# A two-layer cross-attention block: its MLP products in float32r halves, with weight blocks streamed through a ring

## What is computed

```
h = ln(x, ln1);  x = x + attn(rope(h@sa_wq), rope(h@sa_wk), h@sa_wv, causal) @ sa_wo
h = ln(x, ln2);  x = x + attn(rope(h@ca_wq), rope(ctx@ca_wk), ctx@ca_wv) @ ca_wo
h = ln(x, ln3);  x = x + gelu_tanh(h @ fc1_w + fc1_b) @ fc2_w + fc2_b        # MLP of layer 0
a = attn(x@Wq.T, ctx@Wk.T, ctx@Wv.T, causal) + x
a = ln(a, ln_g, ln_b);  out = a + gelu(a @ W1.T + b1) @ W2.T + b2            # MLP of layer 1
```

## Time and profile before

| | |
|---|---|
| median of 3 runs | 1115.44 us (1106.16 to 1116.03) |
| the profiled execution | 1116.21 us, of which the span from first to last instruction is 1114.4 us |
| mean granted TensorE clock | 0.917 of full speed |
| PE / DVE / ACT / POOL busy | 83% / 52% / 38% / 7% |
| DMA | 44.05 MB in packets, mean 40 GB/s |

### The profile page before, as it was taken

The page is one execution under the profiler, slowest core; times in us unless marked ns, Lnnn a source line. Parts: engine busy times, 40 slices in busy tenths (PEclk is TensorE's granted clock), DMA queues, the critical chain, the costliest instruction groups (busy, mean ns, idle before and its releaser), DMA issues.

```text
span 1114.4 us, 13662 instructions
## 1 busy us (share of the span) xinstructions
PE 930.4 (83%) x5120; PEld 456.5 (41%) x5120; DVE 582.7 (52%) x1347; ACT 419.9 (38%) x822; POOL 73.2 (7%) x83
## 2 busy tenths in 40 slices
PE   3878774899988898788989867999887898988898
PEld 1533332345443363344445324533233454543365
DVE  5565727774677604488546775666135515325500
ACT  1233321352455616353422422267752333233421
POOL 2101000000000200000000001000000000000210
PEclk9778866799999998988999988999997999996999
DMA  8804463102122200645020401023004004040000
GB/s 285 101 14 61 83 139 43 16 1 29 27 33 30 29 1 20 95 54 62 1 29 9 50 15 15 20 41 38 1 20 57 2 1 57 2 52 8 1 19 19
DMA packets 47012, 44.05 MB, mean 40 GB/s; under 512 B 13510, under 2 KB 44386, under 8 KB 46434
## 3 DMA queue, kind: packets, MB, share of 16 engines
q1 hardware_dynamic: 46948, 43.19, 24.2%
HBM read 13.53 MB, written 2.10 MB: 14 GB/s over the span
## 4 chain that ended last, share of the span: by engine, by line
PE 57%; DVE 17%; DMA 10%; ACT 7%; SPq 5%; issue 4%; ACTq 0%; DVEq 0%
PE ps_o L963 10%; PE ps_exp L851 10%; PE ps_misc L834 9%; PE ps_max L888 8%; DVE mcol L1113 4%; ACT probs L1199 4%; PE ps_exp L921 4%; SPq L695 4%; DMA QA<-part 4%; PE ps_chain L813 3%; PE ps_chain L821 2%; DVE swap L1027 2%; DMA KA<-part 2%; PE ps_exp L926 2%; PE ps_chain L786 2%
## 5 line engine op out<-in xcount | busy, mean ns | idle before, releaser
L1113 DVE TENSOR_REDUCE mcol<-ps_max 128x3 f32<-128x462 f32 (+5 forms) x496 | 292.1, 626 | 176.7 <-PE ps_max L890 101.0
L1199 ACT ACTIVATE probs<-ps_exp 128x512 f32<-128x512 f32 (+3 forms) x544 | 261.1, 523 | 248.2 <-PE ps_exp L924 90.0
L888 PE MATMUL ps_max<-KA,QA 96*128 96x512 bf16 (+3 forms) x384 | 117.3, 357 | 57.7 <-DVE mcol L1113 27.3
L921 PE MATMUL ps_exp<-QA,KA 98*128 98x512 bf16 (+3 forms) x384 | 119.5, 348 | 27.0 <-ACT probs L1199 18.3
L834 PE MATMUL ps_misc<-hT,w_up 128*128 128x512 f32 x256 | 123.5, 605 | 7.2 <-ACT hid L1190 2.2
L851 PE MATMUL ps_exp<-w_down,hid 128*128 128x256 f32 x512 | 127.7, 386 | 0.0
L1190 ACT ACTIVATE hid<-ps_misc,col 128x512 f32<-128x512 f32 x64 | 44.0, 687 | 196.5 <-PE ps_misc L834 196.5
L851 PEld LDWEIGHTS ps_exp<-w_down,hid 128*128 128x128 f32 x512 | 94.1, 190 | 29.7 <-issue 15.3
L1247 POOL TENSOR_TENSOR part<-rot,part 128x512 bf16<-128x512 f32 (+1 forms) x36 | 40.9, 1135 | 916.3 <-DVE part L1037 916.3
L888 PEld LDWEIGHTS ps_max<-KA,QA 96*128 96x128 bf16 x384 | 39.1, 103 | 126.6 <-DVE mcol L1113 68.2
L963 PE MATMUL ps_o<-probs,V 128*17 128x512 f32 (+3 forms) x768 | 84.2, 512 | 2.9 <-ACT probs L1199 2.0
(11 more groups left out here) (109 smaller groups left out, 986.9 us busy)
## 6 DMA issues: line engine op xcount, KB each, us to landing
QA<-part SPq DMA_DIRECT2D x72, 128.0 KB, 5.2
QC<-part SPq DMA_DIRECT2D x72, 128.0 KB, 5.2
KA<-part SPq DMA_DIRECT2D x48, 128.0 KB, 5.1
xb<-in_x SPq DMA_DIRECT2D x8, 512.0 KB, 6.1
out<-xb SPq DMA_DIRECT2D x4, 512.0 KB, 3.0
KC<-part SPq DMA_DIRECT2D x24, 77.0 KB, 3.0
w_up<-in_fc SPq DMA_DIRECT2D x1, 1024.0 KB, 7.9
w_down<-in_fc SPq DMA_DIRECT2D x1, 1024.0 KB, 8.2
```

The lines of the kernel that those rows point to most:

```text
L888: mm = pe.matmul(dst, q, kk, start=True, stop=not causal)
L921: mm = pe.matmul(bank[:, q0:CH], KA[:, g // NT, hh, (g % NT) * P:(g % NT + 1) * P], QA[:, hh, q0:CH], start=True, stop=(r < 0))
L1113: dve.tensor_reduce(dst, src, AX.X, ALU.max).then_inc(s_max_done, 1)
L1199: act.activation(probs[:, n % 2, h, q0:CH], ps_exp[exp_nth[s] % 2][:, q0:CH], ACT.Exp).then_inc(s_exp_done, 1)
```

## The change

The two MLP products are no longer made of float32 matmuls. Each operand is written as a high half in type float32r plus a low half (the difference), and a product becomes three float32r products: high by high, weight low by input high, weight high by input low.

- Weights: a new thread `split_weights()` with priority -3 (ahead of all others) loads the 16 weight blocks two at a time into `stage`, has ACT write the high halves into `ring` and POOL the low halves, and writes both to a DRAM buffer `keep` (8 rounds of one 512 KB load, one ACT and one POOL operation on 128x1024, one 1 MB store). The loads and stores are issued by ACT's queue, which also waits for them. At the end `fetch` brings the first four blocks (512 KB each) into the ring. The loads of all MLP weights at L645, L646, L670 and L671 are gone.
- Every later block is fetched by SP in the place of a `down`, once that down has released the slot: block n+4 after down n.
- `up`: six products of 128x512 into a bank of `ps_chain`. ACT makes the gelu twice, into `hid` (high, float32r) and into the float32 tile `gel`; POOL subtracts to give the low half, then signals `s_low`. There is one `gel`: the next write waits for POOL.
- `down`: eight products with the high half of `hid`, then after `s_low` four with the low half.
- `tr` of ln3 and ln4: ACT makes four activations in place of two (high half into `hup`, full value into `gel`), POOL the low half. Up 0 waits until ACT has done all of it, and its last two products until POOL has.
- The next MLP's `tr` may stand only after the last up of the MLP before it.
- `lnout` moves from POOL (8 operations) to DVE (2 operations on 128x1024), behind up 0.

```diff
+def split_weights():
+    out = [("wload", 0), ("wload", 1), ("wsplit", 0)]
+    for i in range(NSPLIT):
+        out += [("wsplit", i + 1)] * (i + 1 < NSPLIT) + [("wsave", i)] + [("wload", i + 2)] * (i + 2 < NSPLIT)
+    return out + [("fetch",)]
...
         # SP
-            sp.dma_start(w_up[0][:, :, :], fcw[0]).then_inc(s_wrest, 16)
-            sp.dma_start(w_down[0][:, :, :], fcw[1]).then_inc(s_wrest, 16)
...
-                elif k == "late":
-                    after_chain(sp, ("ctxk", 1, KT - 1))
-                    sp.dma_start(w_up[1][:, :, :], fcw[2]).then_inc(s_wlate, 16)
-                    sp.dma_start(w_down[1][:, :, :], fcw[3]).then_inc(s_wlate, 16)
...
+                elif k == "down" and up_nth[("up", *s[1:])] + RING <= len(ups):
+                    n = up_nth[("up", *s[1:])] + RING
+                    block_used(sp, ups[n - RING - 1])
+                    sp.dma_start(ring[:, n % RING, :, :].bitcast(F32), keep[l * NM + m]).then_inc(s_fetched[n % RING], 16)
...
         # PE
+                    pe.wait_ge(s_fetched[n % RING], 16 * ((n - 1) // RING + 1))
+                    bank = chain_bank(s)
+                    for i, j in ((0, 0), (1, 0), (0, 1)):
+                        if m == 0 and j:
+                            pe.wait_ge(s_low, low_nth[("tr", ("ln3", "ln4")[l], c, NT // 2 - 1)])
                     for t in range(KT):
-                        mm = pe.matmul(bank[:, :], w_up[l][:, t, m * P:(m + 1) * P], hT_of("up", c)[:, t, :],
+                            mm = pe.matmul(bank[:, :], ring[:, n % RING, i, t * P:(t + 1) * P], hup[:, j, t, :],
...
+                    pe.wait_ge(s_gelu, n)
                     for t in range(NT):
-                        mm = pe.matmul(dst, hid[:, m % 2, t * P:(t + 1) * P], w_down[l][:, m, :],
+                        for j in range(2):
+                            pe.matmul(dst[t], hid[:, n % 2, 0, t * P:(t + 1) * P], ring[:, n % RING, j, 2 * P:4 * P],
+                    pe.wait_ge(s_low, low_nth[("up", l, c, m)])
+                    for t in range(NT):
+                        mm = pe.matmul(dst[t], hid[:, n % 2, 1, t * P:(t + 1) * P], ring[:, n % RING, 0, 2 * P:4 * P],
...
         # ACT
+                elif k == "wsplit":
+                    act.wait_ge(s_staged[i % 2], 16 * (i // 2 + 1))
+                    if i > 1:
+                        act.wait_ge(s_saved[i % 2], 16 * (i // 2))
+                    act.activation(ring[:, 2 * (i % 2):2 * (i % 2) + 2, 0, :], stage[:, i % 2, :, :], ACT.Copy)
+                elif k == "wsave":
+                    act.wait_ge(s_wlow, i + 1)
+                    act.dma_start(keep[2 * i:2 * i + 2], ring[:, 2 * (i % 2):2 * (i % 2) + 2, :, :])
...
-                    act.activation(hid[:, m % 2, :], ps_misc[:, :], (ACT.Gelu_apprx_tanh, ACT.Gelu)[l],
+                    act.activation(hid[:, n % 2, 0, :], bank[:, :], gelu, bias=bias).then_inc(s_gelu, 1)
+                    act.wait_ge(s_low, low_nth[s] - 1)
+                    act.activation(gel[:, :], bank[:, :], gelu, bias=bias).then_inc(s_chain_free[u % 2], 1)
...
         # POOL
+                elif k == "up":
+                    after_chain(pool, s)
+                    pool.tensor_tensor(hid[:, n % 2, 1, :], gel[:, :], hid[:, n % 2, 0, :],
+                                       ALU.subtract).then_inc(s_low, 1)
```

225 lines of the change are left out of this document (163 added, 62 removed).

## The result

The changed kernel takes 1097.36 us (median of 14 runs, 1091.97 to 1105.48), the kernel before 1115.28 us (14 runs beside it). The ratio is 0.9849, with a 95% interval of 0.9824 to 0.9873: 1.5% faster. The forecast was 1085 with a range from 1056 to 1116, so the range held and the size was off: 18 us came in place of 31. The executions of one kernel differ by 13 to 17 us, the longer ones mostly at a lower granted clock, so a difference of a few us between two single traces is weak evidence by itself. The profiled execution has a span of 1093.3 us against 1114.4, 21.1 less, and all that follows is read against these 21.1.

What follows compares the result with a forecast made beforehand. PE was taken as the bound, with the MLP's matmuls nearly all on the path. Terms -55 + 11 + 4 + 3 + 2 + 2 + 8 - 6 = -31 took 1116.2 us to 1085, range 1056 to 1116.

Steps and rivals of the forecast that it cites:

- passes, 64 pairs: MLP products on PE: up 1.72 to 1.29 us, down 1.73 to 1.30, over 64 pairs: -55 us.
- heads: Start of each MLP: ACT's extra activations delay up 0, +8 us at seven heads and +3 at the last: +11.
- tails, ring, POOL, lnout: MLP tails waiting for low halves +4, POOL behind DVE +3, ring refills +2, `lnout` on DVE +2.
- prologue and reload: Weight split at the start +8 (ACT +5, KA placement +3), x reload without the two 1 MB loads -6.
- rival 4: Products cheaper than a pass, bounded by bf16's 0.23 us per 512 columns; idleness covers heads and tails: 1066 us, chance 0.12.
- One pass, not two: MLP products: a float32r product takes one pass over its columns; two passes would give over 1200 us, chance 0.02.
- The ring's +2: Block refills during MLPs: they fit by 1.7 us, but a `place` between two holds the second: +2 (0 to 22).
- POOL behind VectorE: First MLP: low half of up 2 stands behind the third part of a projection: +3 us (0 to 6).
- The -6 for the reload: x reload at 150 us: the two 1 MB loads ahead go, 12.42 us against a median of 6.1: -6.
- Rival 1: MLPs: waits for ring refills at the 6.1 us end (+20) eat the gain: 1105 us, chance 0.15.
- Rival 2: Prologue: the weight split fills it, +30 rather than +8: 1107 us, chance 0.10.
- Rival 3: Downs: weight loads bind them, above 0.15 us per product; at 0.216 a down takes 2.59 us: 1164 us, chance 0.07.

Runs made afterwards that it cites:

- e6: Changed kernel with the full-precision input of the MLP heads written into the `hT` slot used before the change, not into `gel`: 1085.62 us, 0.9762.
- e12: Edits of e6, e9 and e10 together, with the halves kept as packed bfloat16 tiles in place of float32r: 1071.72 us, 0.9616.
- e4: Changed kernel without the 60 ring refills; all MLPs read the first four blocks, so the output differs: 1093.1 us, 0.9831.
- e9: On top of e6, in POOL's program alone, a projection's last subtraction goes behind an MLP's next subtraction at two places: 1085.48 us, 0.9769.
- e10: On top of e6, VectorE's two `lnout` operations wait for the low half of the input: 1084.52 us, 0.9749.
- e1: Changed kernel with only four of sixteen weight blocks split, after the second row step, and used by all MLPs: 1093.82 us, 0.982.
- e3: Changed kernel with the weight split of all 16 blocks started behind the second row of maxima of chunk 0: 1101.41 us, 0.9888.
- e11: On top of e6, the planner counts 10 us for a weight load in place of 4, 6 for a save in place of 5: 1087.38 us, 0.9774.
- e5: Changed kernel with MLP products reading only the upper two bytes of each number as bfloat16, four bytes apart: 1092.05 us, 0.9841.

## Why the prediction was right in sign and too large

The sum's terms against what the two traces show, in us of span. The measured heads are the 2.7 of the first, the 9.3 between the MLPs (e6 gives 9.0 of them back, so they are put down to the heads), and 2.7 in the last MLP's stretch (1.19 of waiting and 1.5 at the lower clock). The measured rest is what then remains of the eight stretches.

```
                                     forecast   measured
passes, 64 pairs                       -55       -40.3
heads                                  +11       +14.7
tails, ring, POOL, lnout               +11        -2.7
prologue and reload                     +2        +6.8
end                                      0        +0.4
sum                                    -31       -21.1
```

- **Passes.** This term was mis-sized by 15 us. The step that was off is "That is near enough to 0.108; the ends are 0.108 and 0.216 per product, and I take the first". The distance of 0.12 us in the float32 transposes was the better number: a float32r product of 256 columns takes 0.119 us. It was read as good enough for the ideal, not as the value. Beside the up's 0.232 stood the 0.23 us from one bf16 instruction to the next, a lower bound in rival 4, while the sum used 0.215. That the two agree is in part chance: it bounded nothing from below, since packed bf16 products of 512 columns take 0.216 in e12.
- **One pass, not two: right.** A pair went from 12 instructions in 3.45 us to 18 in 2.82. The Trainium skill ("FP8 and Floating Point Precision", TensorE Precision Notes) has true float32 as four passes and a reduced mode that reads four bytes; the traces agree on the passes (0.86 us for a float32 product of 512 columns, 0.232 for a float32r one). The Trainium skill's 131 ns per pair of load and matmul at 512 columns ("TensorE: Matmul & The Clock Gate", Back-to-back issue gap) is contradicted by the 0.216 us of packed bf16 products, the fastest of 512 columns in any run here.
- **Heads.** Place and size were near, the mechanism was incomplete. The prediction counted ACT's work (+2.3 us a head, half of it covered). It counted the wait on `gel` only for the last head and left out that in the others exponentials are queued behind ACT's wait, and that POOL stands behind VectorE: 3.87 us in the third head. e6 takes away ACT's wait for POOL alone and returns 8.6 us of span. The wait of PE before the last MLP, "some 3 us for ACT `gel`", was 2.54 and 1.19; the fall of the clock behind it was not foreseen.
- **Tails, ring, POOL, lnout.** The ring's +2 is near (2 to 5 in e4), POOL behind VectorE is +3 as forecast (3.1 in e9, clock included), and `lnout` is worth under 1 us (e10). The whole is still negative, and two things blur this row. Counted from start to start in both traces, PE's other work inside the eight stretches takes 36.2 us before and 28.8 after, 7.4 less, though the count of its instructions is nearly the same (255 and 249). Against it stand 17.9 us more at the lower clock, up to 9 us, of which 1.5 are in the row of the heads. The sum had no term for either. They nearly cancel, so with 5 us for the ring and POOL some -8 us of this row stay unexplained; the tails cannot be seen in it, and no run tried them. That this row came out 14 us better than forecast is luck, not foresight: without it the prediction would have been off by 24.
- **Prologue and reload.** "+5 for ACT and +3 for the placement" was 8.7 us for `rot` and 11.5 for SP's queue at the reload; with the reload's -6 taken off it, the row of 6.8 holds some 12.8 for the prologue where the sum had 8. The -6 for the reload is right (the transfer fell by 5.95 us). e1, e3 and e11 put the split later and gained nothing. In e1 the trace shows a collision with the KA placement; in all three PE stood longer at the lower clock before the first up (99.0 and 105.8 us against 88.7 of the changed kernel, 105.8 against 92.2 of e6). Which of the two sets the price, and what a free place would be, stays open.
- **Rivals.** Rival 1 (waits for refills) did not happen: PE has no wait for the ring. Rival 2 (the split fills the prologue) had the right mechanism at about two fifths of its +30 (the 12.8 above). Rival 3 needed more than 0.15 us per product and found 0.119.

## What to carry to other kernels

A rounded-down estimate of a pace is multiplied by every instruction: when the trace has the nearest operand width at a measured distance, take that distance and not the ideal beside it. When a single buffer lets one engine wait for a second whose program is in order, list what each of the two has queued in front and behind; the price here was not the 1.3 us operation alone but the exponentials behind ACT and the projection ahead on POOL. A step's later place in an order moves nothing on an engine that has neither work nor a wait in between. And before a few us between two traces are put down to an edit, read the granted clock of the same stretch in both: here it stood behind 2.9 us of e4's last MLP and part of e9's 3.1.

## What the hardware showed that was not expected

- A product's pace differs with its operands' width and layout: per 256 columns 0.109 us for packed bfloat16, 0.113 for bfloat16 at a stride of four bytes, 0.119 for float32r, while the weight load takes 98, 98 and 193 ns. The Trainium skill ("TensorE: Matmul & The Clock Gate", Weight-path perf modes) says that the fast weight load is on with 128 weights of any type but float32; the loads' two durations agree with it, and the pace between e5 and e12 is not explained by it.
- VectorE and GpSimd hold each other up, and e10, which keeps them apart, takes it away (1.31 us for POOL's subtraction, 1.23 for each of VectorE's operations). In e6 VectorE's first `lnout` operation ran from 1054.55 to 1055.77; POOL's subtraction, begun at 1054.86, ended at 1056.92, 1.15 us behind it; VectorE's second one, begun at 1055.81, took 2.18 us and ended 1.07 us behind POOL's. The Trainium skill ("SBUF — State Buffer", Who interferes with whom) describes an exclusive lock on a port pair for a VectorE operation with two SBUF inputs beside a reading GpSimd; these rows look like it.
- After waits of 2.54 and 1.19 us, eight products ran at 0.43 us each, nearly all of it at the 1.2 GHz level. In e6, with 1.33 and 0.93 us of idleness at the same place, they took 2.11 us, at the 2.4 GHz level. In e4, with the waits of the changed kernel (2.52 and 1.20), the lower level lasted 10.24 us instead of 3.41, and the last MLP was 2.9 us longer: equal waits did not get an equal clock.
